# A graph attention layer on one core: x kept in SBUF, six places for tiles of adj, first load of adj ahead of the centring

## The reference

```python
h = jnp.maximum(_layernorm(x, axis=-1), 0.0)
Wh = h @ W
a1, a2 = (a[:F_OUT, 0], a[F_OUT:, 0])
e = (Wh @ a1)[:, None] + (Wh @ a2)[None, :]
e = jax.nn.leaky_relu(e, negative_slope=0.2)
scores = jnp.where(adj > 0, e, -9e15)
attention = jax.nn.softmax(scores, axis=1)
h_prime = attention @ Wh
return x + jax.nn.elu(h_prime)
```

## Time and profile before

| | |
|---|---|
| Time, median of 3 runs | 671.59 us (671.34 to 671.65) |
| The profiled execution's own time | 671.83 us |
| Its span, first to last instruction | 670.0 us |
| Mean granted clock of PE | 0.989 |
| PE busy | 635.0 us (95%) |
| DVE busy | 619.5 us (92%) |
| ACT busy | 631.1 us (94%) |
| POOL busy | 82.7 us (12%) |
| DMA moved | 141.05 MB, mean 211 GB/s |

### The profile page before, as it was taken

One profiled execution on the slowest core, in us unless ns is written; L12 is line 12 of the kernel. 1 busy time (PEld: TensorE's weight loads), 2 busy tenths in 40 slices (PEclk: granted clock), 3 DMA queues, 4 the chain that ended last, 5 costly groups with the idle time before them and its releaser, 6 DMA issues.

```text
span 670.0 us, 23442 instructions
## 1 busy us (share of the span) xinstructions
PE 635.0 (95%) x10422; PEld 622.4 (93%) x10422; DVE 619.5 (92%) x654; ACT 631.1 (94%) x372; POOL 82.7 (12%) x149
## 2 busy tenths in 40 slices
PE   4878999999999999999999999999899998989997
PEld 4758999999999999999999999999899998989997
DVE  5999999999999999889999999998989989898997
ACT  5799999899999999999999999999899998989982
POOL 7101201101111111000101101010110110101000
PEclk9988999999999999999999999999899999999999
DMA  9999999999999999999999999999999999999980
GB/s 211 217 214 217 215 216 217 217 217 217 218 215 217 217 216 216 218 215 217 216 217 217 216 216 215 218 216 216 217 218 217 215 216 218 215 217 217 216 182 21
DMA packets 32240, 141.05 MB, mean 211 GB/s; under 512 B 3664, under 2 KB 15696, under 8 KB 15952
## 3 DMA queue, kind: packets, MB, share of 16 engines
q0 software_dynamic: 18576, 134.23, 96.0%
q1 hardware_dynamic: 13168, 6.29, 4.2%
q10 hardware_dynamic: 464, 0.07, 0.1%
HBM read 272.70 MB, written 2.10 MB: 410 GB/s over the span
## 4 chain that ended last, share of the span: by engine, by line
ACT 32%; DMA 28%; PE 20%; DVE 11%; issue 7%; POOL 1%; ACTq 0%; DVEq 0%
DMA adj_ring<-in_adj 28%; ACT work L525 23%; ACT work L533 7%; DVE code L728 7%; PE psum L1070 6%; PE psum L1068 6%; PE psum L1048 3%; DVE code L746 1%; PE psum L1037 1%; PE psum L1015 1%; DVE work L752 1%; DMA work<-in_x 1%; PE psum L1005 1%; POOL work L455 1%; ACT last_steps L538 1%
## 5 line engine op out<-in xcount | busy, mean ns | idle before, releaser
L1068 PE MATMUL psum<-V,work 128*128 128x130 f16 x4096 | 492.8, 219 | 0.6 <-DVE work L752 0.5
L1070 PE MATMUL psum<-V,work 128*128 128x130 f16 x4096 | 493.1, 221 | 0.0
L525 ACT ACTIVATE work<-trow,Wh 128x4096 int8<-128x4096 f32 x128 | 477.6, 3735 | 0.0
L1068 PEld LDWEIGHTS psum<-V,work 128*128 128x128 fp8e4 x4096 | 402.2, 98 | 0.9 <-issue 0.9
L1070 PEld LDWEIGHTS psum<-V,work 128*128 128x128 fp8e4 x4096 | 397.8, 97 | 0.0
L728 DVE TENSOR_SCALAR code<-adj_ring 128x4096 uint8<-128x4096 bf16 x127 | 290.5, 2288 | 13.7 <-DMA adj_ring<-in_adj 13.7
L746 DVE SCALAR_TENSOR_TENSOR code<-work,code 128x1024 int32<-128x1024 int32 x128 | 156.6, 1223 | 13.3 <-ACT work L525 11.0
L1048 PE MATMUL psum<-identb,code 128*128 128x128 bf16 x2048 | 137.3, 221 | 17.1 <-DVE code L746 13.7
L533 ACT COPY work<-psum 128x1024 int32<-128x1024 int32 x128 | 130.7, 1024 | 16.0 <-PE psum L1048 15.6
L1048 PEld LDWEIGHTS psum<-identb,code 128*128 128x128 bf16 x2048 | 121.0, 99 | 22.0 <-DVE code L746 11.7
L448 POOL DMA_DIRECT2D adj_ring<-in_adj x127 | 72.3, 570 | 524.7 <-DVE code L728 517.0
(11 more groups left out here) (91 smaller groups left out, 153.7 us busy)
## 6 DMA issues: line engine op xcount, KB each, us to landing
adj_ring<-in_adj POOLq DMA_DIRECT2D x127, 1024.0 KB, 31.8
work<-in_x SPq DMA_DIRECT2D x4, 512.0 KB, 6.2
last_steps<-in_x SPq DMA_DIRECT2D x16, 128.0 KB, 13.9
out_y<-last_steps SPq DMA_DIRECT2D x15, 128.0 KB, 13.9
adj_ring<-in_adj POOLq DMA_DIRECT2D x2, 512.0 KB, 36.0
out_y<-last_steps SPq DMA_DIRECT2D x4, 32.0 KB, 1.5
early_sums<-in_L_gnn_W ACTq DMA_DIRECT2D x4, 16.0 KB, 5.3
a_sb<-in_L_gnn_a ACTq DMA_DIRECT2D x1, 0.5 KB, 4.1
```

What stands on the lines that cost most here:

```text
L525: nc.scalar.activation(sign[:, k % 2].bitcast(I8), trow[:, h * UW:(h + 1) * UW], ACT.Sign, bias=(Wh[:, B, 0:1] if isinstance(B, int) else ...
L1068: nc.tensor.matmul(sums_of[:, 0:FP], up8[:, j // 2, j % 2], V[:, jb, 0:FP], start=begins and j == 0, stop=False, skip_group_check=True)
L1070: last = nc.tensor.matmul(sums_of[:, FP:2 * FP], down8[:, j // 2, j % 2], V[:, jb, FP:2 * FP], start=False, stop=stops and j == HB - 1, sk ...
```

## The change

x is loaded once, into a tensor of its own (`x_sb`), and both the centring and the results read it there; the second load with its semaphore goes, and so does `xg`. The centring writes to `xh` from `x_sb`. `adj_ring` has six places; tile n uses place n modulo 6, and its load waits for the reading of tile n - 6. Both halves of the last tile wait for the reading of tile 121. `adj_ring` and `code` are now views of one tensor, `store`. In POOL's list each of the first four loads stands ahead of the centring of its quarter in place of behind it. DVE waits, before it writes `res`, for the store of the body before. As the places no longer repeat with the bodies, DVE's two loops over bodies are written out. In the general path x is read from `x_sb` too.

```diff
-    RT = 8
+    RT = 6
...
-        adj_ring = sb("adj_ring", [P, RT, TW], BF16)
-        code = sb("code", [P, RM, UW], U8)
+        store = sb("store", [P, 2 * RT * TW + RM * UW], U8)
+        adj_ring = store[:, 0:2 * RT * TW].bitcast(BF16).rearrange("p (t w) -> p t w", w=TW)
+        code = store[:, 2 * RT * TW:].rearrange("p (r w) -> p r w", w=UW)
+        x_sb = sb("x_sb", [P, JB, F])
...
-        last_steps = sb("last_steps", [P, 2 * L_LOW + 2 * L_SUM + 3 * L_BODY])
+        last_steps = sb("last_steps", [P, 2 * RR * FE + 2 * JB])
...
-        xg = part(L_BODY).rearrange("p (k f) -> p k f", f=F)
...
                     for r in range(NR):
-                        sp.dma_start(xh[:, out_of(r), :].rearrange("p (g b) f -> p g b f", b=2),
+                        sp.dma_start(x_sb[:, out_of(r), :].rearrange("p (g b) f -> p g b f", b=2),
                                      xs[:, r * PR:(r + 1) * PR]).then_inc(s_x[r], 16)
 
-                def x_of(i):
-                    sp.dma_start(xg[:, :, :].rearrange("p (w b) f -> p w b f", b=2), x_i[ends[i]]).then_inc(s_xg, 16)
-
-
-                sp.wait_ge(s_lo, 2 * NR)
-                x_of(0)
                 for i in range(NI - 1):
                     sp.wait_ge(s_res, i + 1)
                     sp.dma_start(out_i[ends[i]], res[:, :, :].rearrange("p (w b) f -> p w b f", b=2)).then_inc(s_out, 16)
-
-                    sp.wait_ge(s_pos, i + 1)
-                    sp.wait_ge(s_out, 16 * (i + 1))
-                    x_of(i + 1)
...
-                def load(i, k):
-
-
-                    i, b, h = place(i, k)
-                    pool.dma_start(adj_ring[:, k % RT, :], adj_v[b // 2, b % 2][i, :, h * UW:(h + 1) * UW])\
-                        .then_inc(s_adj[k % RT], 16)
+                def load(n):
+
+
+                    i, b, h = place(n // BU, n % BU)
+                    pool.dma_start(adj_ring[:, n % RT, :], adj_v[b // 2, b % 2][i, :, h * UW:(h + 1) * UW])\
+                        .then_inc(s_adj[n % RT], 16)
 
                 for b in range(NR):
+                    load(b)
                     if b:
                         pool.wait_ge(s_xc, b)
                     pool.wait_ge(s_nm, b + 1)
-                    nc.gpsimd.tensor_tensor(xh[:, out_of(b)], xh[:, out_of(b)],
+                    nc.gpsimd.tensor_tensor(xh[:, out_of(b)], x_sb[:, out_of(b)],
                                             stat[:, 1, out_of(b)].unsqueeze(2).to_broadcast([P, RR, F]), ALU.add)\
                         .then_inc(s_xc, 1)
-                    load(0, b)
-                for k in range(NR, BU):
-                    load(0, k)
-                for i in range(1, NI):
-                    for k in range(BU - 1 if i == NI - 1 else BU):
-                        pool.wait_ge(s_edge, (i - 1) * BU + k + 1)
-                        load(i, k)
-                pool.wait_ge(s_edge, (NI - 1) * BU)
+                for n in range(NR, NI * BU - 1):
+                    if n >= RT:
+                        pool.wait_ge(s_edge, n - RT + 1)
+                    load(n)
+                pool.wait_ge(s_edge, NI * BU - RT)
...
                 def row_sums(b):
                     dve.wait_ge(s_x[b], 16)
-                    nc.vector.reduce_sum(stat[:, 0, out_of(b)], xh[:, out_of(b)], axis=AX.X).then_inc(s_sum, 1)
+                    nc.vector.reduce_sum(stat[:, 0, out_of(b)], x_sb[:, out_of(b)], axis=AX.X).then_inc(s_sum, 1)
...
                     dve.wait_ge(s_T, i * BU + k + 1)
-                    dve.wait_ge(s_adj[k % RT], (i + k // RT) * 16 + 16)
-                    nc.vector.tensor_scalar(code[:, k % RM, :], adj_ring[:, k % RT, :], 0.0,
+                    n = i * BU + k
+                    dve.wait_ge(s_adj[n % RT], n // RT * 16 + 16)
+                    nc.vector.tensor_scalar(code[:, k % RM, :], adj_ring[:, n % RT, :], 0.0,
                                             float(EDGE), ALU.is_gt, ALU.mult).then_inc(s_edge, 1)
...
                 def result(i):
-                    dve.wait_ge(s_xg, i * 16 + 16)
                     dve.wait_ge(s_exp, i + 1)
-                    nc.vector.scalar_tensor_tensor(out=hp, in0=hp, scalar=0.0, in1=xg[:, :, :],
+                    nc.vector.scalar_tensor_tensor(out=hp, in0=hp, scalar=0.0, in1=x_sb[:, ends[i] * KE:(ends[i] + 1) * KE, :],
                                                    op0=ALU.max, op1=ALU.add).then_inc(s_pos, 1)
                     dve.wait_ge(s_pos, i + 1)
+                    if i:
+                        dve.wait_ge(s_out, 16 * i)
...
-                    dve.wait_ge(s_xg, NI * 16)
-                    nc.vector.tensor_tensor(hp[:, b], hp[:, b], xg[:, b], ALU.add).then_inc(z_step, 1)
+                    nc.vector.tensor_tensor(hp[:, b], hp[:, b], x_sb[:, B], ALU.add).then_inc(z_step, 1)
                     after(7)
                     dve.wait_ge(z_exp, b + 1)
+                    if b == 0:
+                        dve.wait_ge(s_out, 16 * (NI - 1))
...
                 body(2, FAR)
-                with dve.Fori(3, CHANGE) as i:
+                for i in range(3, CHANGE):
                     body(i, FAR)
                 body(CHANGE, NEAR, start=FAR - NEAR)
-                with dve.Fori(CHANGE + 1, NI - 1) as i:
+                for i in range(CHANGE + 1, NI - 1):
                     body(i, NEAR)
```

More of the change, by code:

```diff
@@ L56, in build_gat @@
     TR = 8
-    assert UT == 1 and JB % (2 * NR) == 0 and JB % KE == 0 and 2 * F == P and HP % 2 == 0 and RT == UT * BU
+    assert UT == 1 and JB % (2 * NR) == 0 and JB % KE == 0 and 2 * F == P and HP % 2 == 0
     ctx = ExitStack()
@@ L238, in Y @@
             return Y_last[:, h] if r == NR - 1 else V32[:, out_of(min(r + 2, NR - 1)), h]
-        ring = adj_ring[:, :, :].rearrange("p t w -> p (t w)")
-        A = ring[:, 0:2 * N].bitcast(I32)
-        probT = ring[:, 2 * N:4 * N].bitcast(F32)
+        A = store[:, 0:4 * N].bitcast(I32)
+        probT = store[:, 4 * N:8 * N].bitcast(F32)
         score = flat
         Wh1 = V[:, :, :].rearrange("p j v -> p (j v)").bitcast(F32)[:, 0:JB * FE].rearrange("p (j f) -> p j f", f=FE)
-        xt, hpt, negt, rest = xg[:, 0], hp[:, 0, :], neg[:, 0], res[:, 0]
+        hpt, negt, rest = hp[:, 0, :], neg[:, 0], res[:, 0]
         acc1 = psum[:, 0, 0:FE]
@@ L361, in general_vector @@
                         dve.wait_ge(g_fin, i * 2 + 2)
-                        dve.wait_ge(g_x, i * 16 + 16)
                         dve.wait_ge(g_out, ONE + i * 16)
-                        nc.vector.tensor_tensor(rest, hpt, xt, ALU.add).then_inc(g_res, 1)
+                        nc.vector.tensor_tensor(rest, hpt, x_sb[:, bass.ds(i, 1), :].rearrange("p o f -> p (o f)"), ALU.add).then_inc(g_res, 1)
         def general_tensor(pe):
@@ L454, in _ @@
                     pool.wait_ge(s_nm, b + 1)
-                    nc.gpsimd.tensor_tensor(xh[:, out_of(b)], xh[:, out_of(b)],
+                    nc.gpsimd.tensor_tensor(xh[:, out_of(b)], x_sb[:, out_of(b)],
                                             stat[:, 1, out_of(b)].unsqueeze(2).to_broadcast([P, RR, F]), ALU.add)\
                         .then_inc(s_xc, 1)
-                    load(0, b)
-                for k in range(NR, BU):
-                    load(0, k)
-                for i in range(1, NI):
-                    for k in range(BU - 1 if i == NI - 1 else BU):
-                        pool.wait_ge(s_edge, (i - 1) * BU + k + 1)
-                        load(i, k)
-                pool.wait_ge(s_edge, (NI - 1) * BU)
+                for n in range(NR, NI * BU - 1):
[3 more added lines that the diff above has]
+                pool.wait_ge(s_edge, NI * BU - RT)
+                last = (NI * BU - 1) % RT
                 _, b, h = place(NI - 1, BU - 1)
-                for n, loaded in enumerate((s_adj[RT - 1], z_half)):
-                    pool.dma_start(adj_ring[:, RT - 1, n * TW // 2:(n + 1) * TW // 2],
+                for n, loaded in enumerate((s_adj[last], z_half)):
+                    pool.dma_start(adj_ring[:, last, n * TW // 2:(n + 1) * TW // 2],
                                    adj_v[b // 2, b % 2][NI - 1, :, h * UW + n * TW // 2:h * UW + (n + 1) * TW // 2])\
@@ L733, in last_edges @@
                     k = BU - 1
+                    last = (NI * BU - 1) % RT
                     dve.wait_ge(s_T, NI * BU)
-                    for n, loaded, count, written in ((0, s_adj[k], NI * 16, z_edge), (1, z_half, 16, s_edge)):
+                    for n, loaded, count, written in ((0, s_adj[last], (NI * BU - 1) // RT * 16 + 16, z_edge), (1, z_half, 16, s_edge)):
                         part = slice(n * UW // 2, (n + 1) * UW // 2)
                         dve.wait_ge(loaded, count)
-                        nc.vector.tensor_scalar(code[:, k % RM, part], adj_ring[:, k, part], 0.0, float(EDGE),
+                        nc.vector.tensor_scalar(code[:, k % RM, part], adj_ring[:, last, part], 0.0, float(EDGE),
                                                 ALU.is_gt, ALU.mult).then_inc(written, 1)
```

(2 more changed lines are left out.)

8 lines of the change are left out of this document (1 added, 7 removed).

## The result

| | before | changed kernel |
|---|---|---|
| Median of the runs side by side | 671.62 us (671.34 to 671.75, 4 runs) | 676.75 us (676.15 to 677.65, 4 runs) |
| Profiled execution, span | 671.83, 670.0 us | 676.73, 674.9 us |
| Granted clock of PE, mean | 0.989 | 0.988 |

The ratio is 1.0079 (95% interval 1.0067 to 1.0091): slower by 5.1 us, where 1.4 us less was forecast. The time lies 3.5 us above the top of the range.

A forecast was written before the change was run, and what follows sets the result against it. The adj DMA stream was taken to bound the kernel, compute catching it near 450 us. Stream 5.0 - 6.6 + 0.2 = -1.4 us ruled over compute's -12.2 + 10.2 = -2.0, taking 671.59 to 670.2 us; range 663.0 to 673.3.

The forecast's parts named there:

- part 2: Prologue: tile 0 loaded ahead of the centring delays x; everything from the second centring on is 10.2 us later.
- The hold that I expected on the second quarter: Prologue: tiles 0 and 1 hold x's second load until 17.6 us; DVE reads it at 6.68 before.
- The turns of one packet each: DMA queues: adj and x alternate one packet for one, an adj packet taking 0.54 us, 18 times one of x.
- rival A: Prologue: x not held by tile 0, shift 1 us, tile 27 never waits; 663.4 us; chance 0.19 together with another rival.
- The shift: Prologue: everything from the second centring on 10.2 us later, bounds 1 and 15 us.
- Rival B: Prologue moves by 13 us or more, slow PE adding 2 to 5 us; 673.2 us at +3; chance 0.13.
- Part 3, six places: adj stream: load 27 waits for the reading of tile 21 and lands at 156.2, making the stream 5.0 us late.
- Part 1, x: adj stream: no second load of x; 13 remaining loads at 0.51 us each take 6.6 us off.
- The new wait for a store: DVE before writing results: waiting for the previous body's store costs 0, at worst 2 us.
- Part 4, loops: DVE's loops written out: fetching the code costs the stream 0 to 0.5 us, 0.2 taken.
- The sum: Whole kernel: stream -1.4 us at the last tile, compute -2.0; the later, the stream, rules, giving 670.2 us.
- compute floor: Compute at the end: 12.2 us of slack against a 10.2 us later prologue, so -2.0 us.

The follow-up runs named there:

- experiment 8: Changed kernel with loads 0 and 1 of adj ahead of the centring, loads 2 and 3 behind theirs: 672.79 us, ratio 1.0015.
- experiment 2: Kernel before with only the first four loads of adj moved ahead of the centring; eight places, x loaded twice: 676.12 us, ratio 1.0075.
- experiment 4: Changed kernel with load 0 alone ahead of the centring, loads 1 to 3 behind theirs: 671.92 us, ratio 0.9997.
- experiments 1: Changed kernel with the first four loads of adj behind the centring again; six places, x loaded once: 664.48 us, ratio 0.9898.
- experiment 3: Changed kernel with the first loads of adj behind the centring and the second load of x back; six places: 671.94 us, ratio 1.0008.
- experiment 7: Kernel before with DVE's two loops over bodies written out and nothing else: 672.32 us, ratio 1.0011.

## Why the prediction was wrong, point by point

**The failed step is the working of part 2**, "load 0, issued at 2.6, begins to move near 4.1", and with it "load 2 can't be issued meanwhile, so x's third and fourth loads pass in that gap". I took 1.5 us from issue to first packet, which load 0 needs in the kernel before. Here it took 3.4 us: the first packet came just before 6 us, and most of tile 0 later. So x's second quarter was not held at all: row sum at 6.62, not 17.6. But then the second centring was not late either, POOL got to load 2 at 10.41, and this put a third tile beside x's third quarter, which was held to 23.3 by three tiles. The hold that I expected on the second quarter, two tiles long, fell on the third, three tiles long. A favourable fact (load 0 starts late) led to a worse end, because POOL's list let the next loads out. The turns of one packet each, on which it rested, were right: 374 against 470, the even counts in single microseconds, and experiment 8's step of one tile. The Trainium skill has 9 to 17 descriptors to a turn ("DMA: Bandwidth & Descriptors", Queues, rings and completion order). I read this as speaking for rival A, and that was a slip: equal turns of any length hold x just as long on average, and only turns of one queue longer than those of the other would free it. Long turns are told from short ones in short windows. An engine that took nine packets of adj in a row would give x nothing for 9 x 0.54 = 4.9 us and then pass nine of x at once, so over sixteen engines the count of x would jump from one half microsecond to the next; the two windows above have 12 or 13 packets of adj and 11 or 12 of x. So this case's trace does not agree with turns of 9 to 17, as far as sums over the engines can tell; the profile does not name the engine of a packet. The same page's rule to issue a DMA early, which I named beside rival A, would have had the loads ahead; in experiment 2, where that was the only change, it cost 4.7 us.

**The shift** was 13.8 us in place of 10.2. Rival B named this size ("13 us or more"), but by another way: a slow PE. PE was not the cause in the changed kernel (it was part of it in experiment 4). Its third round of transposes started 13.9 us late and took what it took before; the fourth started 13.8 us late (17.99 before):

```profile
27.23 1.94 PE L991 MATMUL psum<-ident,work 128*128 128x128 f32 x8 [0.41 <-ACT V L479]
...
31.81 1.04 PE L991 MATMUL psum<-ident,work 128*128 128x128 f32 x8
```

The same row of the kernel before has 13.32 and 1.96 us. So the lateness was complete when PE got its work, and at tile 21 it was still 13.8.

**Part 3, six places.** Its rule was right, load 27 waiting for tile 21, with the issue 2.6 us after the read: 149.79 and 152.37. With the shift of 13.8 the predicted issue would have been 152.4. The landing took 8.9 us, not 7.4. So the stream's lateness was 10.1 in place of 5.0: 3.6 from the shift, 1.5 from the landing. "Had the prologue not moved, six places would cost nothing" was right: experiments 1 and 3, and the 0.5 against 8.2 of the table.

**Part 1, x.** 15 loads took 7.46 us, 0.50 each; I had 0.51 each, and 6.6 us for the 13 behind tile 27, where 5.9 came between tile 27 and tile 126. Right. The new wait for a store was not tried alone; experiment 3 has it too and stands 0.5 us over the kernel before with all it adds, so it costs no more than that.

**Part 4, loops.** 0.2 us taken, at most 0.5; measured 0.8, 0.1 to 1.3 by the interval. Small, but undersized, and in the wrong place: I put it on the stream, and experiment 7 shows it in compute, behind the last whole tile.

**The sum.** With what was measured the sum holds: stream 10.1 - 5.9 = +4.2 us at the last whole tile, compute floor -12.2 + 13.8 = +1.6, and the later of the two rules, as said. The span of the profiled execution grew by 4.9, so 0.7 us come behind the last whole tile. "After the last tile the work is the same" left them out; the written-out loops alone, in experiment 7, cost 0.6 us in the same place. The range broke at its upper end because I bounded the shift at 15 us in words, and yet gave the whole range only 3 us above the forecast: a shift of 13.8 alone, by the text's own rule of one us of lateness for one us of shift, is 670.2 + 3.6 = 673.8, and was already outside. What it should have had is the case where the second quarter slips through and the third is held, at its own price: three tiles.

## What to carry to other kernels

A small transfer that starts the critical path must be through before large ones are issued on another queue, or share their queue and stand ahead of them: queues share by packets, so 64 short packets an engine beside 8 KB ones waited here for one, two or three tiles, as many as had been issued. Moving a load ahead costs nothing only if the engines are idle at that time; here x had them at a share of 109.5% from 4 to 9.5 us, so there was nothing to win by it. And buffers taken away are free only as long as their reader is not late; cost a ring together with whatever else delays its reader, since here 0.5 us became 8.2.

## What the hardware showed that I had not expected

The time from the issue of a load to its first packet is not fixed. Load 0, issued at 8.13 in the kernel before, had its first packet 1.5 us later; issued at 2.56 in the changed kernel it took 3.4 us, with one packet before 6 us and 14 by 7. x had the engines in both cases (queue 1 at 118.6% from 8 to 9.5 us in the kernel before), so their being full does not explain it alone. The cause was not separated.

On POOL's queue the profile shows x in pieces of 4 KB, 9 packets an engine for each quarter, where SP's queue has 65; the source lines are the same. Issuing a quarter still costs POOL 0.93 us (3.70 for four), against 0.56 to 0.63 us for each of the first four tiles of 1,024 KB in the same run.

PE's granted clock fell further for the same work. The stretch from 45 to 60 us of the kernel before has 0.77, with PE busy 9.93 of 15 us; in the changed kernel the one from 59 to 74 us, 14 us later, has 0.66 and 10.92. ACT is busy 15.00 us in both, so this cost nothing here; its cause was not tried.
